# Two attention layers on one core: each row tile adds into both output banks in turn, and native key chunks are shared out unevenly over the stages

## The reference

```python
q = einsum('rc,bcn->brn', Wq, xf) + bq      # 16 rows
k = einsum('rc,bcn->brn', Wk, xf) + bk      # 16 rows
v = einsum('oc,bcn->bon', Wv, xf) + bv      # 128 rows
attn = softmax(einsum('bri,brj->bij', q, k), axis=2)
out = einsum('bcj,bij->bci', v, attn)
x = gamma * out + x
```

## Time and profile before

| | |
|---|---|
| Median of 3 runs | 206.59 us |
| The profiled execution's own time | 206.91 us |
| Its span | 205.0 us |
| PE busy | 192.7 us, 94% |
| ACT busy | 161.0 us, 79% |
| POOL busy | 155.9 us, 76% |
| DVE busy | 144.8 us, 71% |
| Mean granted TensorE clock | 0.978 of full |

### The profile page before, as it was taken

One profiled execution on the slowest core, in us unless ns is written; L12 is line 12 of the kernel. 1 busy time (PEld: TensorE's weight loads), 2 busy tenths in 40 slices (PEclk: granted clock), 3 DMA queues, 4 the chain that ended last, 5 costly groups with the idle time before them and its releaser, 6 DMA issues.

```text
span 205.0 us, 3349 instructions
## 1 busy us (share of the span) xinstructions
PE 192.7 (94%) x1217; PEld 124.8 (61%) x1217; DVE 144.8 (71%) x146; ACT 161.0 (79%) x237; POOL 155.9 (76%) x88
## 2 busy tenths in 40 slices
PE   7999999999889998999999999999999899998792
...
POOL 1330000686499999998978988999999999999990
...
DMA packets 3746, 9.31 MB, mean 45 GB/s; under 512 B 532, under 2 KB 916, under 8 KB 3732
## 3 DMA queue, kind: packets, MB, share of 16 engines
...
...
## 4 chain that ended last, share of the span: by engine, by line
PE 51%; ACT 15%; POOL 15%; DVE 9%; issue 6%; DMA 2%; SPq 0%; POOLq 0%; DVEq 0%; ACTq 0%
PE out_psum L570 20%; POOL attn_lo L310 10%; PE ring L535 8%; ACT ring L344 7%; ACT attn L362 6%; PE out_psum L600 5%; POOL attn_hi L305 4%; PE out_psum L571 4%; DVE neg_max L435 4%; PE ring L521 4%; PE ring L511 3%; PE ring L556 3%; DMA qk_swapped<-qk 2%; PE ring L499 2%; DVE x_all L460 1%
## 5 line engine op out<-in xcount | busy, mean ns | idle before, releaser
L310 POOL TENSOR_TENSOR attn_lo<-attn,attn_hi 128x1024 fp32r<-128x1024 f32 x48 | 116.2, 2441 | 8.9 <-ACT attn_hi L369 8.0
L435 DVE TENSOR_REDUCE neg_max<-ring 128x1 f32<-128x1024 f32 x64 | 76.5, 1220 | 14.3 <-PE ring L537 13.5
L344 ACT ACTIVATE ring<-ring,neg_max 128x1024 f32<-128x1024 f32 x64 | 69.7, 1088 | 13.1 <-DVE neg_max L435 12.4
L362 ACT ACTIVATE attn<-ring 128x1024 f32<-128x1024 f32 x64 | 63.5, 1024 | 15.8 <-PE ring L558 15.4
L305 POOL TENSOR_SCALAR attn_hi<-attn 128x1024 fp32r<-128x1024 f32 x32 | 36.2, 1138 | 27.9 <-ACT attn L362 27.4
L556 PE MATMUL ring<-qk,qk_swapped 64*128 64x512 f32 x64 | 30.1, 485 | 2.7 <-ACT attn L362 2.0
L570 PE MATMUL out_psum<-attn_hi,v_hi 64*128 64x512 f32 x96 | 30.7, 399 | 1.5 <-DVE x_all L463 1.2
L571 PE MATMUL out_psum<-attn_hi,v_hi 64*128 64x512 f32 x96 | 30.7, 399 | 0.0
L558 PE MATMUL ring<-qk_swapped,qk 64*128 64x512 f32 x64 | 30.5, 491 | 0.0
L570 PE MATMUL out_psum<-attn,v 64*128 64x512 f32 x64 | 30.0, 588 | 0.0
L571 PE MATMUL out_psum<-attn,v 64*128 64x512 f32 x64 | 30.0, 588 | 0.0
...
## 6 DMA issues: line engine op xcount, KB each, us to landing
...
qk<-shift_rows SPq DMA_DIRECT2D x7, 8.0 KB
qk_swapped<-shift_rows SPq DMA_DIRECT2D x7, 8.0 KB
```

The costliest lines, as they stand in the source:

```text
L310: nc.gpsimd.tensor_tensor(attn_lo[:, k - 1], attn[:, k], attn_hi[:, k - 1].bitcast(fp32), ALU.subtract).then_inc(lo_made, 1)
L344: nc.scalar.activation(e[:], e[:], ACT.Exp, bias=max_column(s, i), accum_out=row_sum[s][:, i:i + 1]).then_inc(sum_made, 1)
L362: nc.scalar.activation(attn[:, k], ring_tile("ET", s, k)[:].rearrange("p (a n) -> p a n", a=2), ACT.Exp).then_inc(attn_made, 1)
L435: nc.vector.tensor_reduce(max_column(s, i), ring_tile("E", s, i)[:], axis=AX.X, op=ALU.max, negate=True).then_inc(max_made, 1)
```

## The change

The output banks become the halves: bank 0 holds queries 0 to 511, bank 1 the rest. A slot is now one key chunk of 128 against all 1024 queries. Its product has two parts. Part X sends the lower row tile into bank 0 and the upper into bank 1; part Y sends the lower into bank 1 and the upper into bank 0. The tables name them `HX`, `HY` (v_hi and v_lo times hi) and `PX`, `PY` (v_hi times lo, or the native product). Both row tiles add into both banks, so `finish` is one addition a half, and it waits for the whole stage. A part must not start while the other kind is still adding: every product waits for the last earlier product of the other kind (`part_mm`, in `add_product`).

The native chunks of a stage become a list, `NATIVE = [4, 3, 2, 1, 1, 1, 1, 2]`: 15 native chunks and 49 cut ones, where there were 16 and 48. `v_hi` and `v_lo` are made on POOL, 4 to 7 chunks a stage; 12 of the 49 `lo` are made on DVE, 37 on POOL; 15 `hi` on ACT and 34 on POOL. Stage 0 no longer makes its shift in halves. All five tables are written anew; of them one row stands below.

```diff
-PAIRS = [0, 1, 2, 3, 1, 2, 3, 0]
+
+NATIVE = [4, 3, 2, 1, 1, 1, 1, 2]
+FEWEST = min(NATIVE)
+CUT = TILES - FEWEST
 SLOTS = TILES // 2
-NATIVE = 2
-CUT = TILES - NATIVE
 RING = 3
...
-BY_HALVES = (0,)
+BY_HALVES = ()
...
-raw.0.0.0 raw.0.1.1 QK.1.0.2 E.0.2.0 E.0.1.1 warm.0.8 E.0.0.2 E.0.3.0 warm.0.2 E.0.4.1 warm.0.1 E.0.5.2 E.0.7.0
...
+raw.0.0.0 raw.0.1.1 E.0.0.2 E.0.1.0 QK.1.0.1 E.0.2.2 E.0.3.0 warm.0.8 E.0.7.2 warm.0.3 E.0.6.1 V.0.0.0 E.0.4.2
...
-def half_of(k):
-    return slice(k // SLOTS * HALF, (k // SLOTS + 1) * HALF)
-
-
-def native(k):
-    return PAIRS[k] == 0
+def native(s, k):
+    return k < NATIVE[s]
 
 
...
+        def wait_for_product(engine, s, slots):
+
+            last = [use for use in product_uses if use[0][0] == "P" and use[1] == s and use[2] in slots][-1]
+            engine.wait_ge(part_mm[last[0][1]], nth_part[last])
...
+            def make_v_hi(s):
+                p = s % V_LIVE
+                pool.wait_ge(v32_made, nth_v32[s, 0])
+                nc.gpsimd.tensor_scalar(v_hi[p][:, NATIVE[s] - FEWEST:], v32[p][:, NATIVE[s]:], 1.0, 0.0, ALU.mult,
+                                        ALU.add).then_inc(cut_made["v_hi", "gpsimd"], 1)
+
+            def make_v_lo(s):
+                p = s % V_LIVE
+                wait_for_cut(pool, "v_hi", s, 0)
+                nc.gpsimd.tensor_tensor(v_lo[p][:, NATIVE[s] - FEWEST:], v32[p][:, NATIVE[s]:], v_hi[p][:, NATIVE[s] - FEWEST:].bitcast(fp32),
+                                        ALU.subtract).then_inc(cut_made["v_lo", "gpsimd"], 1)
...
+            def attn_lo_of(s, k):
+                wait_for_cut(dve, "hi", s, k)
+                nc.vector.tensor_tensor(attn_lo[:, k - FEWEST], attn[:, k],
+                                        attn_hi[:, k - FEWEST].bitcast(fp32),
+                                        ALU.subtract).then_inc(cut_made["lo", "vector"], 1)
...
             def finish(s, h):
-
-                dve.wait_ge(pv_mm, all_of(nth_pv, s, range(SLOTS * h, SLOTS * (h + 1))))
+                wait_for_product(dve, s, range(TILES))
                 gamma, part = columns[:, GAMMA + layer(s):GAMMA + layer(s) + 1], slice(h * HALF, (h + 1) * HALF)
-                to = x_all[:, s + B if s < B else s, part]
-                nc.vector.scalar_tensor_tensor(out=to, in0=out_psum[:, 0:HALF], scalar=gamma, in1=x_all[:, s, part],
-                                               op0=ALU.mult, op1=ALU.add).then_inc(x_half_made, 1)
-                dve.wait_ge(x_half_made, nth_finish[s, h])
-                nc.vector.scalar_tensor_tensor(out=to, in0=out_psum[:, HALF:N], scalar=gamma, in1=to,
-                                               op0=ALU.mult, op1=ALU.add).then_inc(x_made, 1)
+                nc.vector.scalar_tensor_tensor(out=x_all[:, s + B if s < B else s, part], in0=out_psum[:, part],
+                                               scalar=gamma, in1=x_all[:, s, part], op0=ALU.mult,
+                                               op1=ALU.add).then_inc(x_made, 1)
...
-                to, part = ring_tile("ET", s, k), half_of(k)
-                first, second = (slice((2 * PAIRS[k] + n) * P, (2 * PAIRS[k] + n + 1) * P) for n in range(2))
-                pe.wait_ge(shift_placed[s][k // SLOTS if s in BY_HALVES else 1], 32)
+                to, rows = ring_tile("ET", s, k), slice(k * P, (k + 1) * P)
+                pe.wait_ge(shift_placed[s][1], 32)
                 wait_for_ring(pe, "ET", s, k)
-                nc.tensor.matmul(to[:, 0:HALF], k_over_q[0:64, first], q_over_k[0:64, part],
+                nc.tensor.matmul(to[:, 0:HALF], k_over_q[0:64, rows], q_over_k[0:64, 0:HALF],
                                  start=True, stop=True)
-                nc.tensor.matmul(to[:, HALF:N], q_over_k[64:128, second], k_over_q[64:128, part],
+                nc.tensor.matmul(to[:, HALF:N], q_over_k[64:128, rows], k_over_q[64:128, HALF:N],
                                  start=True, stop=True).then_inc(et_mm, 1)
 
 
...
-            def add_product(use, passes):
-                _what, s, k = use
-                same = [other for other in products if other[1] == s and other[2] // SLOTS == k // SLOTS]
+
+
+
+            def add_product(what, s, k, passes):
+                first, *_others, last = [use for use in product_uses if use[1] == s]
+                upper, lower = (slice(0, HALF), slice(HALF, N)) if what[1] == "X" else (slice(HALF, N), slice(0, HALF))
+                earlier = [use for use in product_uses[:product_uses.index((what, s, k))] if use[0][1] != what[1]]
+                if earlier:
+                    pe.wait_ge(part_mm[earlier[-1][0][1]], nth_part[earlier[-1]])
                 for n, (v, a) in enumerate(passes):
-                    start = use == same[0] and n == 0
-                    stop = use == same[-1] and n == len(passes) - 1
-                    nc.tensor.matmul(out_psum[:, 0:HALF], v[0:64], a[0:64], start=start, stop=stop)
-                    last = nc.tensor.matmul(out_psum[:, HALF:N], v[64:128], a[64:128], start=start, stop=stop)
-                return last
-
...
+            def wait_for_out(s):
+                wait_for_cut(pe, "v_lo", s, 0)
+                if s > 0:
+                    pe.wait_ge(x_made, all_of(nth_finish, s - 1, range(2)))
+
+            def times_v_high(what, s, k):
+                p, c = s % V_LIVE, k - FEWEST
+                wait_for_out(s)
+                wait_for_cut(pe, "hi", s, k)
+                add_product(what, s, k, [(v[p][:, c], attn_hi[:, c]) for v in (v_hi, v_lo)])
+
+            def times_v(what, s, k):
+                p = s % V_LIVE
+                if native(s, k):
+                    wait_for_out(s)
                     pe.wait_ge(attn_made, nth_attn[s, k])
-                    passes = [(v32[p][:, n], attn[:, k, n]) for n in range(2)]
+                    passes = [(v32[p][:, k], attn[:, k])]
                 else:
-                    pe.wait_ge(lo_made, nth_lo[s, k])
-                    passes = [(v_hi[p][:, c + n], attn_lo[:, k - 1, n]) for n in range(2)]
-                add_product(("PV", s, k), passes).then_inc(pv_mm, 1)
+                    wait_for_cut(pe, "lo", s, k)
+                    passes = [(v_hi[p][:, k - FEWEST], attn_lo[:, k - FEWEST])]
+                add_product(what, s, k, passes)
```

More of the change, by code:

```diff
@@ L55 @@
+PX.7.2 PY.7.2 PY.7.5 PY.7.3 PY.7.7 PY.7.6 PY.7.4
 """
 ACT_ORDER = """
[L57 to L60 removed]
@@ L66 @@
[L66 to L68 removed]
+sum.0.0 sum.0.1 sum.0.2 sum.0.3 sum.0.7 sum.0.6 sum.0.4 sum.0.5 log.0.1 sum.1.5 sum.1.1 sum.1.4 sum.1.0 attn.0.2
+attn.0.0 sum.1.3 sum.1.2 sum.1.7 attn.0.4 attn.0.1 attn.0.3 attn.0.6 sum.1.6 log.1.1 attn.0.5 sum.2.1 attn.0.7
```

212 lines of the change are left out of this document (108 added, 104 removed).

## The result

The changed kernel takes 208.45 us (median of 5 runs, 207.75 to 208.69); the kernel before, run again beside it, 206.85 us (206.31 to 208.1). The ratio is 1.006, with a 95% interval of 1.0032 to 1.0088: 0.6% slower. The forecast was 204.9 us, 0.8% faster, with 62% for faster. Its range held the time, its direction was wrong.

A forecast was written before the change was run, and what follows sets the result against it. PE and POOL were taken to bind together. PE's own work -0.1, start -3.0, waits between parts +3.9, additions -1.0 and late stages -1.5 sum to -1.7 us, giving 204.9 us; range 200.0 to 209.0 us.

The forecast's parts named there:

- The start: Stage 0: first product at 34.6 us, POOL's first hi near 41, stage 0's last remainder ending near 55.5.
- The cause given for the late first product of before: Stage 0 before: first product waits until 43.01 us for the v_lo that DVE makes at 40.73 for 2.23 us.
- Between 5.1 for PE and 1.0 for POOL I take the middle, -3.0: After the start: PE ahead by 5.1 us, POOL by 1.0; the gain booked is -3.0 us.
- POOL's balance: POOL's work left after stage 0: 134.4 us before, now 136.2 plus some 4 for DVE's lo; POOL ahead by 1.0.
- The prediction's own sign of failing: Forecast falls if the first product is later than 37 us or PE waits over 1 us for POOL in middle stages.
- Late stages, -1.5: Stages 6 and 7: POOL gets 4 and 2 lo instead of 6 each, DVE takes seven; -1.5 us, between 0 and -4.
- DVE against POOL: DVE's 12 lo contend with POOL for SBUF: 5 to 7.5 us added, of which 4 booked in POOL's balance.
- third rival: DVE's remainders each stop POOL for up to 2.0 us; time 209 to 211 us, chance 0.13.
- The waits between parts, +3.9: PE's 51 changes of part: 32 at 0.10 us and 2 at 0.33 us, +3.9 us, between 0 and 16.8.
- The second rival: Each of 51 changes of part drains PE at 0.33 us, 217.8 us; at 0.20, 211 us; chance 0.14.
- The additions, -1.0: DVE's finish falls from 32 half additions to 16, and PE waits less for it: -1.0 us, between 0 and -1.4.
- ACT at nothing: ACT loses eight v_hi and one hi; busy 161.0 us, it isn't the bound, so costed at nothing.

The follow-up runs named there:

- experiment 4: Kernel before, with stage 0's cut of v made on idle POOL instead of ACT and DVE: 207.39 us, ratio 0.999.
- experiment 1: Changed kernel with part Y sent through the row tiles as part X is, so no product waits for the other part: 207.46 us, ratio 1.0003.
- experiment 6: Changed kernel with chunk 1 native in stages 4 to 6 and no waits between parts: 203.92 us, ratio 0.9824, against 0.9903 with the waits.
- Experiment 3: Changed kernel with v_hi of stages 1 to 7 back on ACT instead of POOL: 209.54 us, ratio 1.0087.

## Why the prediction was wrong

**The start: right in its numbers.** 34.91, 41.42 and 55.2 us were forecast as 34.6, 41 and 55.5. The cause given for the late first product of before was wrong (experiment 4), and the stretch at the lower clock in before was not in the estimate; how much of the agreement is luck isn't known.

**"Between 5.1 for PE and 1.0 for POOL I take the middle, -3.0": this step failed.** A chain that ends behind POOL gets POOL's advance, not a mean of two engines. PE had its lead, 4.8 us as late as stage 3, and was held to POOL's pace in the end. POOL's balance was forecast well: 152.9 us of work from its first copy on against 151.6 busy us from 41.42 on, and an advance of 1.0 us against 0.7. Its idle time behind the last remainder of stage 0 hardly changed, 5.4 us before and 5.6 after. The sum also left out what stands behind POOL's last remainder, +1.7 us. The prediction's own sign of failing came: PE waited 1.58 us for POOL at 163.83.

**"Late stages, -1.5": wrong in sign.** Fewer `lo` for POOL in stages 6 and 7 was read as relief. Seven of them were given to DVE, where each holds POOL. From stage 3 to stage 6 the change lost 4.9 us instead of gaining 1.5. With short remainders on DVE the same stages lose 1.0 us, so 3.9 of the 4.9 go with the holds (up to 1.4 us of them by way of the clock's dip behind the wait).

**DVE against POOL: the mechanism was named, its weight was missed.** It stood in the third rival with a chance of 0.13 and 209 to 211 us; 208.45 came out. Its "against", that a v_lo cost POOL 0.65 us, is a number for 768 columns in one place. Shortening ten remainders took 9.0 us from POOL, 0.9 each, where the text had 0.87 (0.65 x 4/3) to 1.26. The size of the hold was right. What was missing is that POOL was the bound where six of the twelve stand, in stages 4 to 6, and four more stand behind them, so that most of it counts: 5.5 of 9.0 us. The rule of the Trainium skill that stood beside it (SBUF — State Buffer, "SBUF: two separate sides": of a DVE instruction with two SBUF inputs and a GpSimd instruction that reads SBUF, whichever starts first has the shared pair for the whole instruction, and the other fully blocks) agrees with the 64 columns that take 2.18 and 2.39 us beside a remainder and 0.22 alone. That one of them was held through several of POOL's instructions in a row, 6.88 us, it doesn't say.

**The waits between parts, +3.9: the single wait was too cheap, the sum too high.** With one pair between, the next product starts 0.54 us after the last pass (median of 24 after cut chunks in the trace), and 0.45 where the part stays. That is 0.10 more, where the forecast had 0.03; the pass after it is late by the forecast 0.07. A single wait costs PE 0.17 us, not 0.10, and 32 of them would be 5.4 us, an estimate. Removing all waits gave 1.2 us (experiment 1) and 1.6 us where PE bounds (experiment 6). In experiment 1 part of the rest comes back as waiting for POOL; in experiment 6 where it goes wasn't separated. The second rival, 12.9 us more than the forecast, is out.

**The additions, -1.0: nothing came.** PE's wait in the middle of the last stage, 1.22 us at 194.54 in before, is gone. But that stage now ends behind POOL, and PE waits for it instead, 0.45 us at 191.15 and 0.52 at 199.55. The wait between stages 6 and 7 stayed: the first product starts 1.7 us behind the additions (186.94 and 185.22), as in before (186.81 and 185.11).

**ACT at nothing:** right where nothing was added. Experiment 3, with 4 us more on ACT, didn't get faster though POOL was 6.5 us lighter, so the opposite may not be free.
